# Attention scores and row maxima from 58-row float32r stacks in two halves of TensorE's rows, in place of 115-row bfloat16 stacks

## What is computed

```
scores = einsum('bhid,bhjd->bhij', q, k) / sqrt(16)
scores = scores - |i - j| * 0.5**h
attn   = softmax(scores, axis=-1)
out    = einsum('bhij,bhjd->bhid', attn, v)
```

## Time and profile before

| | |
|---|---|
| runs | 1685.29 us median of 3 (1679.18 to 1689.55) |
| profiled execution | 1684.55 us |
| its span | 1682.7 us |
| TensorE busy (by the profile's modelled ends) | 1617.6 us, 96% |
| VectorE busy | 1024.9 us, 61% |
| ScalarE busy | 785.5 us, 47% |
| GpSimd busy | 320.9 us, 19% |

### The profile page before, as it was taken

The page is one execution under the profiler, slowest core; times in us unless marked ns, Lnnn a source line. Parts: engine busy times, 40 slices in busy tenths (PEclk is TensorE's granted clock), DMA queues, the critical chain, the costliest instruction groups (busy, mean ns, idle before and its releaser), DMA issues.

```text
span 1682.7 us, 29721 instructions
## 1 busy us (share of the span) xinstructions
PE 1617.6 (96%) x10022; PEld 966.9 (57%) x10022; DVE 1024.9 (61%) x2366; ACT 785.5 (47%) x1635; POOL 320.9 (19%) x310
## 2 busy tenths in 40 slices
PE   5889999999999999999999999989999999999996
PEld 2333334344454444445434453379998999989996
DVE  4888887888777778877788775423444233232322
ACT  3046656667546666655675657842221212212121
POOL 6100120002200041210031100331341212212121
PEclk9789999999999999999999999999999999999998
DMA  6921540233140440323421613335666666566653
GB/s 172 158 67 35 96 80 13 31 42 58 48 78 27 73 80 8 45 59 82 67 57 38 141 51 102 115 105 148 179 194 195 181 183 183 164 181 165 184 163 74
DMA packets 92660, 173.30 MB, mean 103 GB/s; under 512 B 13235, under 2 KB 51123, under 8 KB 92384
## 3 DMA queue, kind: packets, MB, share of 16 engines
q1 hardware_dynamic: 75376, 143.69, 34.4%
q0 software_dynamic: 15744, 26.54, 7.3%
q10 hardware_dynamic: 1392, 1.18, 0.3%
HBM read 133.69 MB, written 37.29 MB: 102 GB/s over the span
## 4 chain that ended last, share of the span: by engine, by line
PE 89%; DVE 3%; ACT 3%; DMA 3%; issue 2%; ACTq 0%; POOL 0%; SPq 0%; POOLq 0%; DVEq 0%
PE ps L1057 15%; PE ps L1272 14%; PE ps L1249 14%; PE ps L1083 14%; PE ps L1043 13%; PE ps L1113 3%; DVE rmax L1427 2%; PE ps L1135 2%; PE ps L1122 2%; PE ps L1104 2%; PE ps L1169 2%; PE ps L1046 2%; PE ps L1086 2%; ACT prob L1290 1%; DMA out<-yo,xi 1%
## 5 line engine op out<-in xcount | busy, mean ns | idle before, releaser
L1427 DVE TENSOR_REDUCE rmax<-ps 128x1 f32<-128x512 f32 x1024 | 665.0, 685 | 197.7 <-PE ps L1083 96.3
L1290 ACT ACTIVATE prob<-ps 128x512 f32<-128x512 f32 x1024 | 559.6, 601 | 326.9 <-PE ps L1046 177.4
L1083 PE MATMUL ps<-stacked_k,stacked_q 112*128 112x512 bf16 x1024 | 397.2, 391 | 10.9 <-DVE rmax L1427 8.3
L1043 PE MATMUL ps<-stacked_q,stacked_k 115*128 115x512 bf16 x1024 | 359.0, 383 | 5.0 <-ACT prob L1290 3.2
L1057 PE MATMUL ps<-prob,values 128*32 128x512 f32 x2048 | 273.7, 606 | 5.3 <-ACT prob L1290 5.3
L1249 PEld LDWEIGHTS ps<-xiT,w_now 128*128 128x128 f32 x2272 | 266.2, 193 | 3.4
L1249 PE MATMUL ps<-xiT,w_now 128*128 128x128 f32 x2272 | 267.7, 276 | 0.0
L1272 PE MATMUL ps<-w,hidT 128*128 x1136 | 260.2, 382 | 7.7 <-issue 7.3
L1083 PEld LDWEIGHTS ps<-stacked_k,stacked_q 112*128 112x128 bf16 x1024 | 100.4, 98 | 285.7 <-DVE rmax L1427 208.5
L1396 ACT ACTIVATE hidT<-ps,b 128x128 f32<-128x128 f32 x284 | 81.1, 368 | 354.8 <-PE ps L1249 354.8
L1272 PEld LDWEIGHTS ps<-w,hidT 128*128 128x128 f32 x1136 | 210.2, 190 | 40.9 <-issue 14.7
(11 more groups left out here) (181 smaller groups left out, 1130.0 us busy)
## 6 DMA issues: line engine op xcount, KB each, us to landing
w_now<-in_w SPq DMA_DIRECT2D x71, 1024.0 KB, 5.5
stacked_q<-parts_of_rows SPq DMA_DIRECT2D x90, 128.0 KB, 6.6
stacked_k<-parts_of_rows SPq DMA_DIRECT2D x90, 128.0 KB, 7.2
xi<-expert_rows SPq DMA_DIRECT2D x71, 130.0 KB, 2.1
w<-in_w SPq DMA_DIRECT2D x8, 1024.0 KB
parts_of_rows<-q_part SPq DMA_DIRECT2D x21, 256.0 KB, 8.8
parts_of_rows<-k_part SPq DMA_DIRECT2D x21, 256.0 KB, 9.0
xr<-in_x POOLq DMA_DIRECT2D x4, 1024.0 KB, 9.2
```

The source lines that it names most:

```text
L1043: m = e.matmul(ps[:, bank, :], ka[i][0:ROWS, hh, kt * P:(kt + 1) * P], qa[i][0:ROWS, hh, ch * BANK:(ch + 1) * BANK], start=True, stop=True)
L1083: m = e.matmul(ps[:, bank, :], qa[i][0:MAX_ROW, hh, qt * P:(qt + 1) * P], ka[i][0:MAX_ROW, hh, kc * BANK:(kc + 1) * BANK], start=True, sto ...
L1290: e.activation(prob[:, u % NPROB, :], ps[:, score_bank(u), :], ACT.Exp).then_inc(sem["exp"], 1)
L1427: e.tensor_reduce(rmax[:, G % 2, hh * NT + qt, kc:kc + 1], ps[:, p.bank("max", *k), :], AX.X, ALU.max).then_inc(sem["maxed"], 1)
```

## The change

- Queries and keys are split in two parts of type float32r, a 4-byte type (`high` by ScalarE, `low` by one VectorE instruction); `rest`, `mid` and GpSimd's part of the work fall away. Three pairs of parts, 48 rows, 8 rows of positions (now in one part each) and 2 rows of maxima make stacks of 56 rows (max) and 58 rows (score).
- Even heads have their stack in partitions 0 to 63, odd heads in 64 to 127, so that a product uses half of the array's rows.
- The planner keeps two lists of maxima, of even and of odd heads. A unit first tries a maximum of the half that its score does not use, then the score, and then the ramps of both, as steps of their own. The chance for a maximum at the end of a unit is gone; the two behind the score stay.
- The spreads, position rows and maximum rows are now issued by GpSimd, with twice the number of DMAs for each tensor part (one for each half): 14 for a spread, 4 for the rows of maxima (3 before). The rounding of the position rows through DRAM at the start falls away; they are read straight from the input.
- `TAKES` has new costs: score 0.14, max 0.14 and each ramp 0.1 us (before: 0.26 for either product with its ramp).
- `xn_next` is gone (the normalised rows overwrite `xr_next`), so the next batch is fetched after its turn, not after its norm. A few waits of the start and of the plan move (`FIRST_ALONE`, `pause(12)`).

```diff
-NPART = 3
-PAIRS = [(0, 0), (0, 1), (0, 2), (1, 0), (1, 1), (2, 0)]
+NPART = 2
+HALF = P // 2
+NJ = HG // 2
+PAIRS = [(0, 0), (0, 1), (1, 0)]
+NPOS = 2 * NSUB
+MAX_ROW = NPOS + len(PAIRS) * DH
 ROWS = MAX_ROW + NPART
...
-    "pe": {"score": 0.26, "max": 0.26, "attend": 1.03,
+    "pe": {"score": 0.14, "max": 0.14, "score_ramp": 0.1, "max_ramp": 0.1, "attend": 1.03,
...
     def row_maxima(G):
-        for hh, qt, kc in maxima_of(G):
+        left = [maxima_of(G, odd) for odd in range(2)]
+        while left[0] or left[1]:
+            odd = now["odd"] if left[now["odd"]] else 1 - now["odd"]
+            now["odd"] = 1 - odd
+            hh, qt, kc = left[odd].pop(0)
             add("max", G, hh, qt, kc)
+            if qt // 4 == kc:
+                if now["pairing"]:
+                    ramps.append(("max_ramp", G, hh, qt, kc))
+                else:
+                    add("max_ramp", G, hh, qt, kc)
             add("maxed", G, hh, qt, kc)
...
         def unit(ch, kt, hh):
+            now["odd"], now["pairing"] = 1 - hh % 2, True
+            maximum(0)
+            now["pairing"] = False
             add("score", G, ch, kt, hh)
+            while ramps:
+                add(*ramps.pop())
+            if kt // 4 == ch:
+                add("score_ramp", G, ch, kt, hh)
             add("exp", G, ch, kt, hh)
...
                         step_on(closing)
                         behind(G // NG)
-                    maximum(0)
...
+        stacked = lambda odd, first, last: slice(HALF * odd + first, HALF * odd + last)
+        pair_rows = lambda odd, j: stacked(odd, NPOS + DH * j, NPOS + DH * (j + 1))
+        rows_at = lambda stack, rows, hh, cols: stack[stacked(hh % 2, 0, rows), hh // 2, cols]
...
-                    m = e.matmul(ps[:, bank, :], ka[i][0:ROWS, hh, kt * P:(kt + 1) * P],
-                                 qa[i][0:ROWS, hh, ch * BANK:(ch + 1) * BANK], start=True, stop=True)
+                    m = e.matmul(ps[:, bank, :], rows_at(ka[i], ROWS, hh, run(kt, P)), rows_at(qa[i], ROWS, hh, run(ch, BANK)), start=True, stop=True)
...
-                    m = e.matmul(ps[:, bank, :], qa[i][0:MAX_ROW, hh, qt * P:(qt + 1) * P],
-                                 ka[i][0:MAX_ROW, hh, kc * BANK:(kc + 1) * BANK], start=True, stop=True)
+                    m = e.matmul(ps[:, bank, :], rows_at(qa[i], MAX_ROW, hh, run(qt, P)), rows_at(ka[i], MAX_ROW, hh, run(kc, BANK)), start=True, stop=True)
...
+                elif kind == "spread":
+                    G, = k
...
+                    for j, (of_q, of_k) in enumerate(PAIRS):
+                        for odd in range(2):
+                            rows = pair_rows(odd, j)
+                            e.dma_start(qa[i][rows, :, :], by_row(stage[b % 2, 0, of_q, heads, :], odd)).then_inc(sem[f"spread{i}"], 16)
+                            e.dma_start(ka[i][rows, :, :], by_row(stage[b % 2, 1, of_k, heads, :], odd)).then_inc(sem[f"spread{i}"], 16)
+                    key_position_rows(G, sem[f"spread{i}"])
+                elif kind == "max_rows":
+                    G, = k
+                    e.wait_ge(sem["nrow"], G + 1)
+                    for n in range(NPART):
+                        for odd in range(2):
+                            e.dma_start(qa[G % NSET][stacked(odd, MAX_ROW + n, MAX_ROW + n + 1), :, :],
+                                        nparts[run(odd, NJ * NT), n, :].bitcast(F32)).then_inc(sem["max_rows"], 16)
```

More of the change, by code:

```diff
@@ L75 @@
 TAKES = {
-    "pe": {"score": 0.26, "max": 0.26, "attend": 1.03, "av_turn": 0.45, "max_turn": 0.12, "turn": 0.45, "proj": 0.86, "vproj": 0.86, "out": 0.86,
+    "pe": {"score": 0.14, "max": 0.14, "score_ramp": 0.1, "max_ramp": 0.1, "attend": 1.03, "av_turn": 0.45, "max_turn": 0.12, "turn": 0.45, "proj": 0.86, "vproj": 0.86, "out": 0.86,
            "cross": 1.1, "p_turn": 0.45, "cross_out": 1.5, "logits": 0.9, "rank": 0.3, "c_turn": 0.4, "kv": 1.04, "qk": 1.04, "cb": 0.5,
@@ L100 @@
 TABLE_PARTS = 6
-FIRST_ALONE = 5 * UNITS // 8
+FIRST_ALONE = UNITS // 2
 WHOLE, FORE, AFT = (0, NT), (0, NT // 2), (NT // 2, NT)
-EMPTIED = {"max": "maxed", "max_turn": "nrow", "turn": "turned", "proj": "rest", "vproj": "values",
+EMPTIED = {"max": "maxed", "max_turn": "nrow", "turn": "turned", "proj": "low", "vproj": "values",
            "out": "add1", "cross": "cross_max", "p_turn": "p_turned", "cross_out": "add2",
@@ L279, in turn @@
                     p.free["turned", which, b, c, four] = mine[four]
+                while which == "on" and ("on", NG * b + NG - 1, four) not in p.number:
+                    yield 0
                 yield from until("turn", which)
@@ L287, in prepare @@
         yield from layer_norm("pre", b, WHOLE)
+        yield from turn("pre", b, WHOLE)
         if 0 < b < NB - 1:
             add("fetch_next", b + 1)
[L290 removed]
         if b == 0:
@@ L302, in prepare @@
                     add("high", b, mo, a, ch)
-                    for kind in ("rest", "mid", "low"):
-                        empty(kind, b, mo, a, ch)
+                    empty("low", b, mo, a, ch)
                     yield 10
@@ L544, in step_on @@
             parts.pop(0)
-    now = {"unit": 0, "ended": 0, "spread": 0, "maxima": 0, "running": False, "late": False}
+    now = {"unit": 0, "ended": 0, "spread": 0, "maxima": 0, "running": False, "late": False, "odd": 0, "pairing": False}
+    ramps = []
     placing, closing, staging, emptying, scattering = [], [], [], [], []
@@ L601, in plan @@
                 add("late_in")
+        elif ("low", 0, 1, 0, 1) in p.number and not now["maxima"] and not p.open:
+            pass
         elif beside and (p.open or p.room() <= p.pe + 0.3):
@@ new lines, in _ @@
+                    if G == 0 and (qt >= NT // 2 or kc) and "rest of the first rows" not in started:
+                        started.add("rest of the first rows")
+                        e.wait_ge(sem["spread0"], spread_in(0))
+                    bank = side_bank(kind, *k)
+                    m = e.matmul(ps[:, bank, :], rows_at(qa[i], MAX_ROW, hh, run(qt, P)), rows_at(ka[i], MAX_ROW, hh, run(kc, BANK)), start=True, stop=True)
+                    if qt // 4 != kc:
+                        m.then_inc(sem["max"], 1)
+                elif kind == "max_ramp":
+                    G, hh, qt, kc = k
+                    e.matmul(ps[:, p.bank("max", *k), run(qt % 4, P)], slopes[:, G % NG * HG + hh, :], ramps[:, 1 - qt % 2, :],
+                             start=False, stop=True, skip_group_check=True).then_inc(sem["max"], 1)
```

250 lines of the change are left out of this document (98 added, 152 removed).

## The result

| | before | changed |
|---|---|---|
| median, us | 1684.85 | 2204.24 |
| lowest and highest of five runs | 1679.18, 1689.55 | 2189.96, 2250.61 |
| ratio, 95% interval | | 1.3051 [1.3016, 1.3086] |
| profiled execution, us (span) | 1684.55 (1682.7) | 2250.61 (2248.8) |

The account below looks back on a forecast made before the run. TensorE was taken to bound the score stage; -132 (slots) + 152 (changes) + 55 and 12 (loads) + 10 (GpSimd issues) = +97 on 1684.55 us gave 1780, chance 0.48, range 1600 to 1865 (its own 1715 to 1860).

Parts of the forecast that it names:

- At full clock: Attention, 150 to 1000 us of the earlier trace: TensorE busy 840.6 of 850 us at full clock; no clock term.
- Changes of arrangement, +152: TensorE's scores and maxima: 1714 more switches between halves, all rows or column strips at 0.089 us, +152 us.
- Slots, -132: Scores with a max directly ahead: 608 pairs run beside each other, each saving a slot of 0.217 us, -132 us.
- Loads in the open, +55 and +12: First weight load of each of 1041 blocks cannot hide, +55 us; 237 float32 side work pieces, 0.05 each, +12 us.
- Start, 0: Before the first scores: 14 GpSimd issues instead of 13 on two queues, less other work; -3 to +5 us, taken as 0.
- GpSimd's issues, +10: Spreads issued on GpSimd, 14 issues each, delay the layer norms' `rstd` for three batches; bounds 0 and 30, taken +10 us.
- Starved by GpSimd: Rival: each of 16 spreads stops something on TensorE for most of its 10 us, +100 us on 1780; chance 0.05.
- VectorE, 0: VectorE loses 8 us of small `nrow` instructions but does not bound, with TensorE as cover: 0.
- Free halves: Rival: going between all rows and a half needs no drain and hides its loads, 1585 us; chance 0.22.
- no overlap: Rival: the two halves run one after the other, or float32r takes two passes, about 1910 us; chance 0.08.
- All paired, 1680: Rival: a max stands beside practically every score, about 950 slots go, 1680 us; chance 0.17.
- The signs: Trace marks: pair starts 0.01 to 0.1 us apart, ramp 0.4 later, loads 141 ns or more, VectorE idle, at most two thirds paired.

Follow-up runs that it names:

- full_rows: Changed kernel with each product taken on the rows of both halves at once, so no halves or pairs: 1825.63 us, ratio 1.0867.
- before_58: Kernel before, in bfloat16, with scores from rows 0 to 57 and maxima from rows 0 to 55 only: 2311.11 and 2470.03 us.
- micro2: Bare TensorE streams computing nothing of the reference, mixing row counts, ramps, strips and waits; 58 rows (bfloat16) and a ramp took 0.760 us at clock 0.50.
- two_pairs: Changed kernel with a maximum ahead of each score and two units' pairs in succession, their ramps behind all four products: 1912.19 us, ratio 1.1393.
- micro: First kernel of bare TensorE streams, computing nothing of the reference: equal products on fixed tiles without waits, 840.49 us at full clock throughout.
- strip_ramps: Kernel before with each ramp as four products in column strips, same sums: 1869.08 us, ratio 1.1108.
- full_ctx: Changed kernel on the rows of both halves at once, with the context's weight loads issued by SyncE instead of GpSimd: 1823.34 us against 1825.63.
- always_pair: Changed kernel in which each unit puts a maximum ahead of its score whether or not the plan holds a bank free: 1900.54 us, ratio 1.1301.

## Why the prediction was right or wrong

**The step that failed is the one that isn't there.** "At full clock" was read from the earlier trace rows and carried over to the new order; no term and no rival had the clock in it. It is 355 of the 566 us. The rows could have raised the question: the one change of arrangement that I measured leaves 0.09 us gaps, the change was to make over 2000 of them, on half of the rows. What such a stream does to the clock no row of before shows, so it should have stood as an unknown with two ends, the upper at half speed. The cause is shown by removal on both sides: all rows with the same order (full_rows) bring the clock back, bfloat16 with half of the rows in the old kernel (before_58) takes it down, and in the bare stream (micro2) 58 rows need the single half and the gaps together. What exactly it takes within the kernel stays open. The changed kernel's stretches at 1.2 GHz hold 431 lone halves and 222 pairs (products that start within 0.05 us of each other), those at full clock 421 and 339; and two_pairs falls for 195 us with practically no lone half. Which mixtures of lone halves, pairs, attends and waits fall and which don't (500 to 520 us against 560 to 580, above) I have not resolved.

**Changes of arrangement, +152: right.** 0.089 us each holds for halves (micro, both halves and a ramp) and for strips (strip_ramps). Their number came out at 2376 instead of 2224, so 166.

**Slots, -132: right.** 613 pairs are in the new order, 60% of the scores, and some 560 are visible in the trace as starting together; a slot is 0.227, since float32r streams 5% slower: -139. That slower stream on all 2048 products is +22, a term that I did not have.

**Loads in the open, +55 and +12: less than half of what they are.** This is the term of the order's sum that failed. The upper bound of the text, 0.11 each, was nearer: the second product of a block starts 0.335 us behind the first where it would be 0.227. I took the middle because a recorded transpose load (141 ns) seemed nearest; now the record of the scores' loads is 231 ns (183 at full clock). The Trainium skill, TensorE: Matmul & The Clock Gate, section LDWEIGHTS, gives columns over 1.2 GHz, 107 ns for 128; the gap, 0.108, agrees.

The timeline has +194 for the order. With 166 - 139 + 22 = 49 for the other terms, 145 us are left for the loads, where the forecast had 67. That is 0.13 for each of the 1110 blocks, and the pair with its ramp in micro leaves the same: 0.593 - 0.227 - 0.056 - 0.178 = 0.13. The mechanism of the forecast was the right one, for a third of the loss. The forecast's own range was also drawn too narrow: its bounds, the loads at 14 or 111 and 50 to 75% of units paired, give 1666 to 1883 when they come together, not 1715 to 1860.

**Start, 0: wrong by 31.** I counted GpSimd's issues, not what stands behind them: the context's loads are behind the second spread and its wait. About 8 us are that (full_ctx). The rest falls into a stretch at a mean clock of 0.65, where it had been 0.77 (30 to 134 us, and 30 to 103 before); I did not separate it further.

**GpSimd's issues, +10: not seen.** TensorE waits for nothing that the norms hold up, and once for a spread itself (L1070, 5.1 us). An issue of a spread took 0.5 us on GpSimd, not the 0.74 that I read from a weight load's issue. "Starved by GpSimd" is out. **VectorE, 0: right** as long as its banks are free when the order asks for them, and wrong where they are not (always_pair).

**The rivals.** "Free halves" is out (a ramp 0.43 behind the pair, changes at 0.089), "no overlap" too (starts 0.003 apart, two float32r products in 0.227). "All paired, 1680": tried, 1900. Its argument about VectorE was right: the plan's condition for pairing keeps TensorE's waits for VectorE's reductions (200 to 1100 us) at 4.8 us in the changed kernel, where always_pair has 42.0.

**The signs** named ahead were nearly all found: starts together, a ramp 0.43 behind, loads over 141 ns, VectorE idle, 60% paired. They confirm the mechanism of the sum, though not the size of its loads, and none of them could have shown the clock: that needed the PEclk row.

## What to carry to other kernels

Before splitting TensorE's rows into halves, ask what the stream looks like when only one half has work: here a stream rich in lone halves between short full-row products cost more through the clock (355 us) than through its gaps and loads (194). Whoever uses halves should pair nearly all of their products, or leave them on all rows; and even with nearly all of them paired 78 to 250 us of the scores stayed at 1.2 GHz. Price every change of arrangement (0.09 us each way) and every 4-byte weight load behind a short product (0.1) before counting the saved slots; a pair saves 0.22, but a pair and one ramp take 0.59 in float32r, where two bfloat16 products on all rows and a ramp take 0.49. And give the granted clock a term of its own, with both ends, whenever a change alters how much of the array works.

## What the hardware showed that I had not expected

- 58 rows, dense: full clock, 0.216 us per product of 512 columns. 26 rows, dense: 1.2 GHz, 0.427. 58 rows with a ramp between: 1.2 GHz, 0.760 per product and ramp (0.48 before the clock fell), against 0.484 for both halves and a ramp.
- Reading 66 rows instead of 58 in the kernel before is a difference of 607 us and more (1703.68 against 2311.11 and 2470.03).
- With nearly every half paired the clock still falls at times within the kernel: 195 us of two_pairs's scores, with 2 lone halves in them.
- float32r streams in one pass at 0.227 us per 512 columns, 5% above bfloat16; its load is hidden behind another product of 512 columns, and leaves 0.078 us open behind a ramp even without a change of arrangement.
- A ramp as four column strips costs some 0.18 us more than in one piece (182 us for some 1000 of them), which is the way in and out, twice 0.089.
